# Second norm ahead of the router's ranking, one transfer per slot for queries and keys, and a gate unit after the last exponentials, in a fused kernel of token mixing, attention and experts

## The reference, cut to what matters

```python
# 1. image rows: token mixing with exp weights, then a layer norm with gain and bias
y = sigmoid(q) * (ew @ (ek * v)) / (ew @ ek)          # ek = exp(k), ew = exp(w_bias * mask)
h = layernorm(y @ out_w + out_b + flatten(x)) * ln_g + ln_b
h = concatenate([h, take(W_E, x_txt) * 16])           # 384 rows
# 2. attention, 16 heads of 16, with relative positions of at most 4 to each side
n = layernorm(h)
s = q @ k.T + band(q @ rel_k.T);  p = softmax(s);  o = p @ v + band_of(p) @ rel_v
h = h + o @ Wo + bo
# 3. eight experts, all computed for every row, weighted by a router
n = layernorm(h);  inh = sigmoid(n @ Wr / temperature);  dist = abs(inh - 1/e)
w = exp(-dist / 0.1) * in_zone(inh)                   # fallback: the best 2 of exp(-dist / 0.3)
h = h + sum_e w[e] * ((silu(n @ Wg[e]) * (n @ Wu[e])) @ Wd[e])
```

## Time and profile before

| | |
|---|---|
| median of 3 runs | 1242.7 us (1239.78 to 1243.44) |
| the profiled execution | 1242.83 us, of which the span from first to last instruction is 1241.0 us |
| TensorE matmul busy | 1023.4 us (82%) |
| VectorE / ScalarE / GpSimd busy | 751.7 (61%) / 451.2 (36%) / 242.6 us (20%) |
| one round (from one start of turn_outputs to the next, 566.30 to 709.70) | 143.4 us |
| mean granted TensorE clock | 0.949 of full speed |
| HBM traffic | 60.35 MB read, 26.92 MB written |

### The profile page before, as it was taken

How to read it: one execution, slowest core, us unless ns; L and a number is a source line. 1 busy time by engine, 2 the same in 40 slices (tenths; PEclk the granted TensorE clock), 3 DMA queues, 4 the chain that set the end, 5 groups by cost and what they waited for, 6 DMA issues and landing times.

```text
span 1241.0 us, 16784 instructions
## 1 busy us (share of the span) xinstructions
PE 1023.4 (82%) x5668; PEld 745.0 (60%) x5668; DVE 751.7 (61%) x1605; ACT 451.2 (36%) x651; POOL 242.6 (20%) x262
## 2 busy tenths in 40 slices
PE   5446689879898898878898798888898888987798
PEld 4221378628785477636786287745786277762687
DVE  5466364865568556774648655675658746486443
ACT  1134313472235522453134723355124631247211
POOL 4258120040200311031200402013200312004000
PEclk9677799989999999999999999999999899998899
DMA  5394206302081203602062111802044020620100
GB/s 159 120 232 145 40 5 177 62 10 57 6 211 30 39 18 89 148 10 52 4 180 59 31 34 35 202 10 39 18 146 92 10 52 5 180 60 14 40 1 13
DMA packets 96962, 87.87 MB, mean 71 GB/s; under 512 B 67281, under 2 KB 85074, under 8 KB 95090
## 3 DMA queue, kind: packets, MB, share of 16 engines
q1 hardware_dynamic: 96524, 86.24, 28.2%
q0 software_dynamic: 384, 1.05, 0.3%
HBM read 60.35 MB, written 26.92 MB: 70 GB/s over the span
## 4 chain that ended last, share of the span: by engine, by line
PE 34%; issue 23%; DVE 19%; DMA 9%; SPq 5%; ACT 5%; POOL 4%; POOLq 0%; DVEq 0%; ACTq 0%
PE S L924 10%; DMA k_st<-d_parts 6%; DVE maxima L1233 5%; PE S L945 5%; SPq L573 4%; PE S L855 4%; PE S L838 4%; DVE S L1254 3%; PE S L790 3%; PE S L750 3%; ACT scratch L1045 3%; DVE res L1387 2%; PE S L666 1%; DMA txt_row<-in_L_txt_W_E,txt_idx 1%; DMA w_d<-in_L_ffn_Wg 1%
## 5 line engine op out<-in xcount | busy, mean ns | idle before, releaser
L1506 POOL TENSOR_TENSOR bands<-scratch,one 64x432 f32<-64x432 f32 x128 | 119.2, 931 | 529.0 <-ACT scratch L1045 523.4
L1082 ACT ACTIVATE silu<-S 128x384 f32<-128x384 f32 x128 | 62.9, 491 | 371.4 <-PE S L924 260.2
L1233 DVE TENSOR_REDUCE maxima<-S 128x2 f32<-128x768 f32 x192 | 172.7, 951 | 27.3 <-PE S L798 26.2
L945 PE MATMUL S<-w_d,hT 128*128 128x256 f32 x768 | 182.7, 382 | 1.5 <-DVE hT L1375 0.7
L1254 DVE TENSOR_TENSOR S<-S,bands 64x144 f32<-64x144 f32 x384 | 154.4, 402 | 48.1 <-PE S L838 37.5
L1045 ACT ACTIVATE scratch<-S 128x768 f32<-128x768 f32 x192 | 155.4, 811 | 60.4 <-DVE S L1254 45.1
L790 PE MATMUL S<-k_st,q_st 128*128 128x384 bf16 x384 | 102.7, 334 | 65.3 <-DVE maxima L1233 37.1
L945 PEld LDWEIGHTS S<-w_d,hT 128*128 128x128 f32 x768 | 142.4, 190 | 21.7 <-issue 2.3
L1375 DVE TENSOR_TENSOR hT<-silu,S 128x384 f32<-128x384 f32 x128 | 70.7, 552 | 118.6 <-PE S L924 96.9
L838 PE MATMUL S<-q_st,k_st 128*128 128x384 bf16 x384 | 99.9, 360 | 41.7 <-ACT scratch L1045 37.9
L838 PEld LDWEIGHTS S<-q_st,k_st 128*128 128x128 bf16 x384 | 25.8, 100 | 135.3 <-ACT scratch L1045 99.4
(11 more groups left out here) (167 smaller groups left out, 1510.7 us busy)
## 6 DMA issues: line engine op xcount, KB each, us to landing
bands<-d_band_s SPq DMA_DIRECT2D x16, 864.0 KB, 8.8
scratch<-d_band_t SPq DMA_DIRECT2D x8, 1632.0 KB, 8.2
d_parts<-scratch SPq DMA_DIRECT2D x48, 192.0 KB, 1.9
q_st<-d_parts SPq DMA_DIRECT2D x48, 192.0 KB
k_st<-d_parts SPq DMA_DIRECT2D x48, 192.0 KB
d_band_w<-bands SPq DMA_DIRECT2D x32, 240.0 KB, 3.8
out<-scratch SPq DMA_DIRECT2D x8, 384.0 KB, 2.6
x_in<-in_x SPq DMA_DIRECT2D x8, 256.0 KB, 3.3
```

Source lines behind the costliest of these rows:

```text
L945: mm = pe.matmul(D[:, i // 2, (i % 2) * E:(i % 2 + 1) * E], hT[:, (FT * e + m) % 3, i * P:(i + 1) * P], w_d[:, e, m, :], start=(m == 0), s ...
L1233: dve.tensor_reduce(dst, S[:, c0:c0 + 2, PAD:PAD + T], AX, ALU.max).then_inc(max_done.sem, 1)
L1506: nc.gpsimd.tensor_tensor(bands[rows, :, :, 2 * pair:2 * pair + 2].rearrange("p i w h -> p h i w"), win, one[rows].unsqueeze(2).unsqueeze( ...
```

## The change

Four edits. (1) In the mixed section `mix_norm`, `norm_stats` and `turn_norm` come ahead of the router's ranking; the ranking is cut in two steps; gain and bias of the second row tile move from GpSimd to VectorE; `hidden` is put on VectorE ahead of mix_norm and of norm_stats. (2) `hT` gets 4 slots instead of 3, and the units come as four gate/up pairs, then per expert its two down units and the next two pairs. 23 units instead of 25 are placed ahead of the maxima, 10 instead of 9 among them. (3) One DMA per slot brings its query and its key rows (6 DMAs with 32 rows instead of 12 with 16), behind `band_t` and behind all six part writes. (4) One gate unit moves between the last values steps, so one fewer follows turn_outputs ahead of turn_attn.

With these tables a round has, from mix_out on: up 0 (hidden 0), mix_norm, gate 1, up 1 (hidden 1), norm_stats, gate 2, up 2 (hidden 2), gate 3, turn_norm, up 3, router_rank, router_order, router_pick (hidden 3), down 0, project_qk, project_rel, gate 4, up 4, project_v, gate 5, up 5, down 1, pairs 6 and 7, down 2, gate 8, maxima 0 and 1, up 8, maxima 2, gate 9, maxima 3 to 5, up 9, maxima 6 to 8, (down 3, 0), maxima 9 to 11, (down 3, 1), maxima 12 and 13, accumulate (3, 1), negate 0, maxima 14, gate 10, maxima 15 to 17, up 10, maxima 18 to 20, gate 11, maxima 21 and 22, up 11, maxima 23, (down 4, 0), accumulate (4, 0), negate 1, negated 1, (down 4, 1), gate 12, up 12, the attends with gate 13 behind the first of the last three values steps, turn_outputs, up 13, down 5, turn_attn, pairs 14 and 15, down 6, turn_weights, (down 7, 0), rel_values, (down 7, 1). Before, the section from maxima 0 to the attends held (down 3, 1), gate 9, up 9, gate 10, up 10, down 4, gate 11, up 11, gate 12, up 12 and (down 5, 0), with down 4 ahead of maxima 15 and 18.

```diff
 KT = E // P
+HSLOTS = 4
 TXT = 128
...
 FILL_MIX = [("residual", 0), ("mix_in", 0), ("turn_x2", 0), ("mix_sums", 0), ("router", 1),
-            ("mix_out", 0), ("router_zone", 1), ("mix_norm", 1), ("router_rank", 2),
-            ("norm_stats", 2), ("router_pick", 1), ("turn_norm", 2), ("project_qk", 0),
-            ("project_rel", 1), ("project_v", 14)]
-FILL_MAXIMA = [0, 1, 1] + [0, 0, 1] * 7
+            ("mix_out", 0), ("router_zone", 1), ("mix_norm", 2), ("norm_stats", 3), ("turn_norm", 1),
+            ("router_rank", 0), ("router_order", 0), ("router_pick", 2), ("project_qk", 0),
+            ("project_rel", 2), ("project_v", 11)]
+FILL_MAXIMA = [0, 1, 1] + [0, 0, 1] * 6 + [0, 1, 1]
 WEIGHTS_MAXIMA, WEIGHTS_ATTEND = (10, 18), (2, 12)
...
         hid = sb("hid", [P, TT, E])
-        q_st = sb("q_st", [P, AH, T], BF16)
-        k_st = sb("k_st", [P, AH, T], BF16)
+        qk_st = sb("qk_st", [P, 2, AH, T], BF16)
+        q_st, k_st = qk_st[:, 0], qk_st[:, 1]
         v_one = sb("v_one", [P, TT, AH, VC])
...
         silu = sb("silu", [P, T])
-        hT = sb("hT", [P, 3, T])
+        hT = sb("hT", [P, HSLOTS, T])
         stat = sb("stat", [P, TT, 6])
...
-        units = [("gate", 0), ("up", 0), ("gate", 1), ("up", 1)]
+        units = []
+        for n in range(HSLOTS):
+            units += [("gate", n), ("up", n)]
         for e in range(NE):
-            if e + 1 < NE:
-                units += [("gate", 2 * e + 2), ("up", 2 * e + 2)]
-            units += [("down", e, 0), ("down", e, 1)]
-            if e + 1 < NE:
-                units += [("gate", 2 * e + 3), ("up", 2 * e + 3)]
+            parts_e = [("down", e, 0), ("down", e, 1)]
+            n = FT * e + HSLOTS
+            if n < FT * NE:
+                parts_e += [("gate", n), ("up", n), ("gate", n + 1), ("up", n + 1)]
+            units += parts_e
         after = {"up": "hidden", "down": "accumulate"}
...
                 fill(3)
-                steps += [("router_zone",), ("router_rank",), ("router_pick",)]
+                steps += [("router_zone",), ("router_rank",), ("router_order",), ("router_pick",)]
                 fill(len(left))
                 flush()
                 return steps + [("store",)]
             for name, n in FILL_MIX:
+                if name in ("mix_norm", "norm_stats"):
+                    flush()
                 if name not in LATE_STEPS or ffn:
...
             last = AH // GRP - 1
+            if ffn:
+                assert left[0][0] == "gate"
+                steps.append(("gate_bank",))
+                fill(1)
             steps += [("values", last, i, dict(seen)) for i in VALUE_TILES[1:]] + [("copy", last)]
...
-                def stack(st, base, order):
+                def stack():
+                    size = E * T
                     for n in range(SLOTS):
+                        q, k = Q_PART[n], 3 + K_PART[n]
                         sp.dma_start(
-                            st[NEG + n:P:G8].rearrange("p h t -> p (h t)"),
-                            d_parts[base + order[n]].rearrange("(d g) m t -> d (g m t)", d=AD)
+                            qk_st[NEG + n:P:G8].rearrange("p s h t -> p s (h t)"),
+                            dram(d_parts, q * size, (AH * T, AD), ((k - q) * size, 2), (1, AH * T))
                         ).then_inc(stacked.sem, 16)
...
                 sp.dma_start(q_st[0:NEG], d_zero).then_inc(stacked.sem, 16)
-                sp.wait_ge(q_out.sem, q_out.at(b, 3))
-                stack(q_st, 0, Q_PART)
...
+                sp.wait_ge(q_out.sem, q_out.at(b, 3))
                 sp.wait_ge(k_out.sem, k_out.at(b, 3))
-                stack(k_st, 3, K_PART)
+                stack()
                 if not later(b):
...
                         pe.wait_ge(pool_consts, 8)
-                    pe.wait_ge(stacked.sem, stacked.at(b, 2 * SLOTS + 1))
+                    pe.wait_ge(stacked.sem, stacked.at(b, SLOTS + 1))
                     pe.wait_ge(v_done.sem, v_done.at(b, TT))
...
+            def gate_bank(b):
+                pe.wait_ge(o_copied.sem, o_copied.at(b, AH // GRP - 1))
...
                     act.wait_ge(band_t_in.sem, band_t_in.at(b, 1))
+                    act.wait_ge(q_out.sem, q_out.at(b, 3))
                     act.wait_ge(k_out.sem, k_out.at(b, 3))
...
                 norm(b, mix_dve, mix_root, mixed, lambda i: hid[:, i], IT)
+                if not later(b):
+                    dve.wait_ge(loaded[1], 16 * N_LOADS[1])
+                dve.wait_ge(mix_dve.sem, mix_dve.at(b, 5 + 3 * IT))
+                dve.tensor_tensor(hid[:, 1], hid[:, 1], ln_g[:], ALU.mult).then_inc(hid_second.sem, 1)
+                dve.wait_ge(hid_second.sem, hid_second.at(b, 1))
+                dve.tensor_tensor(hid[:, 1], hid[:, 1], ln_b[:], ALU.add).then_inc(hid_second.sem, 1)
...
             def norm_stats(b):
-                dve.wait_ge(hid_ready.sem, hid_ready.at(b, 5))
+                dve.wait_ge(hid_ready.sem, hid_ready.at(b, 3))
+                dve.wait_ge(hid_second.sem, hid_second.at(b, 2))
                 stats(b, ln2, 0, lambda i: hid[:, i], TT)
...
                     dve.wait_ge(band_t_in.sem, band_t_in.at(b, 1))
+                    dve.wait_ge(q_out.sem, q_out.at(b, 3))
                     dve.wait_ge(k_out.sem, k_out.at(b, 3))
...
+            def router_order(b):
+                step = stepper(b, [R_DIST + 7])
+                other = fb.unsqueeze(2).broadcast_to([P, TT, NE, NE])
+                own = fb.unsqueeze(3).broadcast_to([P, TT, NE, NE])
                 step(dve.tensor_tensor(rpair2, other, own, ALU.is_gt))
...
                 dve.wait_ge(up_pe.sem, up_pe.at(f, n + 1))
-                if n >= 3:
-                    dve.wait_ge(down_pe.sem, down_pe.at(f, 2 * ((n - 3) // FT + 1)))
-                dve.tensor_tensor(hT[:, n % 3], silu[:], U[:, 0:T], ALU.mult).then_inc(h_done.sem, 1)
+                if n >= HSLOTS:
+                    dve.wait_ge(down_pe.sem, down_pe.at(f, 2 * ((n - HSLOTS) // FT + 1)))
+                dve.tensor_tensor(hT[:, n % HSLOTS], silu[:], U[:, 0:T], ALU.mult).then_inc(h_done.sem, 1)
...
                     pool.wait_ge(loaded[1], 16 * N_LOADS[1])
-                for i in range(IT):
-                    pool.wait_ge(mix_dve.sem, mix_dve.at(b, 5 + 2 * IT + 1 + i))
-                    nc.gpsimd.tensor_tensor(hid[:, i], hid[:, i], ln_g[:], ALU.mult).then_inc(hid_ready.sem, 1)
-                    pool.wait_ge(hid_ready.sem, hid_ready.at(b, 2 + 2 * i))
-                    nc.gpsimd.tensor_tensor(hid[:, i], hid[:, i], ln_b[:], ALU.add).then_inc(hid_ready.sem, 1)
+                pool.wait_ge(mix_dve.sem, mix_dve.at(b, 5 + 2 * IT + 1))
+                nc.gpsimd.tensor_tensor(hid[:, 0], hid[:, 0], ln_g[:], ALU.mult).then_inc(hid_ready.sem, 1)
+                pool.wait_ge(hid_ready.sem, hid_ready.at(b, 2))
+                nc.gpsimd.tensor_tensor(hid[:, 0], hid[:, 0], ln_b[:], ALU.add).then_inc(hid_ready.sem, 1)
```

More of the change, by code:

```diff
@@ L278, in fusion_block @@
         q_out, k_out = sig("q_out", 3, 16), sig("k_out", 3, 16)
-        stacked = sig("stacked", 2 * SLOTS + 1, 16)
+        stacked = sig("stacked", SLOTS + 1, 16)
         rel_t_out, rel_s_out = sig("rel_t_out", P // BT, 16), sig("rel_s_out", TT, 16)
@@ L952, in _ @@
                         "project_v": project_v, "maxima": maxima, "weights_ready": weights_ready, "negate": negate,
-                        "negated": negated, "attend": attend, "values": values, "turn_weights": turn_weights,
+                        "negated": negated, "attend": attend, "gate_bank": gate_bank, "values": values, "turn_weights": turn_weights,
                         "turn_outputs": turn_outputs, "rel_values": rel_values, "turn_attn": turn_attn,
```

10 lines of the change are left out of this document (5 added, 5 removed).

## The result

The changed kernel takes **1288.5 us** (median of four runs, 1285.4 to 1290.5) against 1241.2 for the kernel before, run beside it: ratio 1.036, 95% interval 1.033 to 1.039. It is slower by 47 us; the forecast was 1268.6 with a range of 1238 to 1282. Direction right, size too small. The profiled execution took 1285.4 us, its span 1283.6 against 1241.0.

What follows compares the result with a forecast made beforehand. TensorE was taken as the bound, its matmuls busy 82% of the span, so idle time decides. +4.0 us a round, +28.0 over seven, -1.4 in round 0 and -0.7 in the tail gave 1268.6 us; range 1238 to 1282.

Steps and rivals of the forecast that it cites:

- the norm's step: Between mixing and project_qk: second norm's transposes start 4.3 us earlier, TensorE waits 2.6 instead of 5.1, project_qk 2.8 earlier.
- The landing: Stacked rows ahead of maxima 0: last landing 647.8 instead of 649.6, maxima 0 1.9 us earlier, TensorE wait 4.7 instead of 1.19.
- Neither is on the path, for the engines are the limit: SyncE's transfer issues: halving 12 issues saves up to 3.6 us or, at the upper bound, nothing; neither affects the path.
- The clock: Start of the maxima: the 4.7 us wait lowers TensorE's clock, 1.1 us a round; bounds 0 or 2.2, longer low 3.5.
- The ends: Attends and round's end: one hidden replaces two accumulates, -0.4 us; down (5, 0) is new in the round's end, +1.7.
- the 4.0: Forecast sum per round: -1.9 + 3.5 - 0.4 + 1.7 + 1.1 = +4.0 us; seven rounds +28.0.
- Round 0: Statistics wait 2.73 us for GpSimd's four instructions, half of which go: -1.4 us.
- The tail: The wait of 0.70 us ahead of down 7 is covered by down 6: -0.7 us.
- (a): Rival: the clock holds and waits are smaller, +2.9 us a round, 1261; without both negate waits 1247; chance 0.21.
- (b): Rival: merged transfers run at band_t's 411 GB/s, maxima 0 starts 6.4 us earlier, -1.6 a round, 1230 us; chance 0.18.
- The upper price for tile 1's gain and bias: On VectorE beside GpSimd's products: 0.78 us per instruction rather than 0.43; product until 609.4, sum until 610.3.
- (c): Rival: nothing measurable; transfers end near 645 or overlooked slack fills the turns' waits, 1239 to 1246.5 us; chance 0.11.

Runs made afterwards that it cites:

- e4: The changed kernel with twelve separate stacking transfers again, the queries' six ahead of band_t and the keys' six behind it: 1277.6 us (1.030).
- e5: The changed kernel with gate 8, the last unit ahead of the maxima, computing its product five times in all rounds but the tail: 1279.1 us (1.032).
- e3: The changed kernel with 14 units behind project_v instead of 11 and no accumulate or second down part next to a turn: 1235.3 us (0.996).
- e7: The changed kernel with 14 units behind project_v, no accumulate or second down part next to a turn, and twelve separate transfers: 1215.5 us (0.980).
- e16: The kernel before with its sixteen-row groups on every seventh partition and nothing else changed: 1250.8 us (1.008).
- e1: The changed kernel with three units moved from between the first maxima to behind project_v (14 there instead of 11): 1271.8 us (1.024).
- e2: The changed kernel with units among the maxima placed so that no accumulate or second down part stands next to a turn: 1254.1 us (1.010).
- e13: The changed kernel with each slot's sixteen rows on every seventh partition instead of every eighth, in both stacks: 1274.0 us (1.028).
- e12: The kernel before with the six merged transfers alone, behind band_t and all six part writes: 1258.0 us (1.012).
- e14: The kernel of e7 with its rows on every seventh partition: 1228.1 us (0.990).

## Why the prediction was right or wrong

**Right, within 0.3 us:** the norm's step. Laid over the trace of before, the second norm's transposes start at 614.49 (forecast 614.75), project_qk at 618.85 (619.1), band_t is issued at 630.46 (630.5). Also the units' end (643.10, forecast 643.3) and the wait's place, and at the second turn both waits (0.97 and 1.23 us, forecast 1.0 and 1.35). The first turn's 2.21 us is TensorE's; VectorE stands idle 1.18 of it, where the forecast had a delay of 1.0. The rows move at 224 GB/s, just above the 200 to 220 of the forecast. Two slips did no harm: the eleven units' own terms add up to 12.35 us, not 12.8, and one ranking instruction took 1.89 us beside GpSimd, not 0.8, with cover enough.

**The landing, 0.6 us off:** maxima 0 at 648.70 (forecast 648.1), a wait of 5.6 us (4.7). The term that was off is "17.3 us from first issue to last landing", kept from the old form: it is 18.0. More weighty is what it hid. The forecast gave the merged form the 2.8 us of the earlier projections and found maxima 0 1.9 us earlier; e4 shows that with separate transfers it would have come 1.8 us earlier still (B to C 28.0 instead of 29.9). "Neither is on the path, for the engines are the limit" was wrong for the 1.6 us in which the queue stood and the engines were half idle.

**The clock, the term that was mis-sized, and the step that failed:** taken at 1.1 us a round, it was 3.4 in the maxima. From C to D the forecast had 35.2 without the clock; e5's one round with no low stretch took 35.5. The changed kernel takes 38.9, two low stretches more (38.9 - 35.5 = 3.4). I priced one stretch, by half of the old one in the attends, and saw none at the turns, though I had written down their three waits. The bound of 3.5 named for "a longer low" was the place to be; it gives 1285 us, and the range stopped at 1282. The forecast also left out what the clock gives back. The kernel before has a low stretch in the attends of every round, the changed kernel in none, and such a stretch has a price too: D to A is 27.9 us without one and 28.7 to 29.3 with one (e3, e7). The kernel before would take about 27 there at a full clock (26.9 in the last round of e16, the one round of its form with no low stretch; an estimate), so about 1 us a round came back, and the clock's net cost is some 2.4.

**The ends:** the attends and the round's end cost 0.8 us (D to A -0.1, A to up 0 +0.9), forecast 1.3. That is near by luck: about 1 us of clock, which no term had, came off work that cost some 1.8. For round 4 the sum is 0.6 (landing) + 2.6 (C to D, clock included) - 0.5 (ends) above the 4.0: 6.7 us, and 6.8 was measured (150.17 against 143.40). Over the seven rounds it is 38.7, not 47, because round 4 of the kernel before, which stood for all, was among its three shortest; its mean is 144.5. Round 0 was forecast at -1.4 and came out at +2.1 (head): the norm's wait was 1.1 us shorter, its start only 0.15 earlier, and the rows' wait rose from 18.3 to 20.5, which the forecast of the landing hadn't applied to it. The same round 0 has 18.8 to 19.2 there in e1, e2, e3 and e5, so one execution doesn't settle this term. The tail was forecast at -0.7 and came out at +1.7: the wait of 0.70 did fall to 0.20, but 0.95 us of work moved behind the last A. The clock is low as long as before, only later, in the third to fifth ten us (0.80, 0.69, 0.83; before 0.65, 0.67, 1.00); whether the rest comes from that is not shown. 38.7 + 2.1 + 1.7 is the span's 42.5 us. Of the 20 us between forecast and median, 10.7 are the seven rounds, 5.9 the head and the tail, and 3.1 that the profiled execution is the fastest of the four.

**The rivals.** (a) fell with the clock. (b) had the merged rows run at band_t's rate: they ran at 224. What it says of band_t's 128 partitions was to the point: e13 gets up to 301 GB/s out of the same transfers by the place of their rows. The rule of larger DMAs (the Trainium skill, DMA: Bandwidth & Descriptors, Bandwidth) doesn't show here: 384 KB moved at 224 GB/s, 192 KB at 203 to 217, where the prediction's estimate from its table had 18% less time. The page measured that table with transfers to 128 partitions, these go to sixteen. The upper price for tile 1's gain and bias was right: on VectorE they took 0.62 and 0.85 us beside GpSimd's, and ended within 0.05 us of the forecast. (c) had no support.

## What to carry to other kernels

When work is taken out of the stretch that covers a transfer, price two things: the wait, and the low clock behind it; then look for short waits further on in the same phase, which bring a stretch of their own. Before merging two transfers, ask what the queue and the engines do in the time in which the first of them moved alone. Look for low stretches that a change takes away, too. Take cover and place of the units as one question: here two lists of counts were worth 53 us, and with the transfers left separate the same change is 26 us faster than the kernel before instead of 47 slower.

## What the runs showed of the hardware

- **A low stretch has nearly a fixed price within one phase here.** C to D goes from round to round in steps: 30.4 or 32.1 us (e3), 35.5, 37.1 or 38.7 (e5), 1.6 us for each stretch; 1.3 in e12 and e16 (31.7 or 33.0). A stretch in the attends costs 0.7 to 1.5 us (27.9 or 28.7 to 29.5, e3, e4 and e7). In e1 and e2, whose stretches differ in length, the steps are less clean.
- **Which waits brought one.** Over the seven rounds of all eighteen kernels, a low stretch stood at the start of the maxima behind all 59 waits of more than 3.0 us for the rows, behind 16 of 23 between 2.0 and 3.0, and behind none of 44 shorter ones. Taking one away can call up another one later (e5).
- **The place of sixteen rows bears on their DMA rate:** 125 GB/s adjacent, 217 on every eighth partition, up to 301 and 233 in the mean on every seventh, 424 for band_t on all 128. The Trainium skill (SBUF — State Buffer, Door 1: The DMA port swizzle) gives a partition's port by bits 2 to 4 and 6 of its number; by it these reach 5, 8, 14 or 15, and 16 of 16 ports. The order agrees, and so do two of the sizes: by that page's ports, 5/16 of 424 is 132, a half 212, both estimates. Every seventh gets less than its share, which would be 371 or more, so the 300 that the expectation of e13 put down as that page's isn't what its ports give. The forecast didn't weigh that page.
- **A higher rate in one part is not an earlier landing:** in the four us from 1.0 us behind its first query issue e14 moves 267 GB/s, e7 240; at the end of its key rows e14 moves 206 and 143, and B to C is 1.2 us longer than e7's.
